# Sparse mixtures: routing two blocks ahead of the scatters, positions in a PSUM bank of their own, two blocks routed in the prologue

## The reference

```
x = x + 0.5 * L0_ffn(layernorm(x))      # gated mixture
x = x + L0_attn(layernorm(x))           # 16 heads, segments of 32 with a memory
x = x + 0.5 * L0_ffn(layernorm(x))      # the gated mixture again, same weights
x = x + 0.5 * L1_ffn(layernorm(x))      # SiLU mixture
x = x + L1_attn(layernorm(x))           # 8 heads in a band
x = x + 0.5 * L1_ffn(layernorm(x))      # the SiLU mixture again
```

```
# L0_ffn, gated (F = 128)
scores = softmax(xt @ gate_w.T)
idx    = top_k(scores + gate_b, 2)                   # weights = scores[idx]
h      = (xt @ w1[e].T + b1[e]) * (xt @ w3[e].T + b3[e])
y      = swiglu(h) @ w2[e].T + b2[e]                 # the shared expert likewise
# L1_ffn, SiLU (I = 512)
gates  = softmax(relu(xf @ Wr1 + br1) @ Wr2 + br2)
tg, ti = top_k(gates, 2);  tg = softmax(tg / 2)
h      = silu(xf @ We1[e] + be1[e]) @ We2[e] + be2[e]   # the shared expert likewise
```

## Time and profile before

| | |
|---|---|
| runs | 2786.85, 2788.24, 2788.27 us; median 2788.24 |
| profiled execution | 2785.44 us, its span 2783.6 us |
| granted TensorE clock, mean | 0.814 of full speed |
| busy: PE | 2066.6 us, 74% of the span |
| busy: DVE | 1942.6 us, 70% |
| busy: ACT | 1387.4 us, 50% |
| busy: POOL | 1102.2 us, 40% |

### The profile page before, as it was taken

How to read it: one execution, slowest core, us unless ns; L and a number is a source line. 1 busy time by engine, 2 the same in 40 slices (tenths; PEclk the granted TensorE clock), 3 DMA queues, 4 the chain that set the end, 5 groups by cost and what they waited for, 6 DMA issues and landing times. The chain is left out here.

```text
span 2783.6 us, 86687 instructions
## 1 busy us (share of the span) xinstructions
PE 2066.6 (74%) x35134; PEld 1660.7 (60%) x35134; DVE 1942.6 (70%) x4609; ACT 1387.4 (50%) x2243; POOL 1102.2 (40%) x885
## 2 busy tenths in 40 slices
PE   3688399999999998569578975755666555549894
PEld 2577378887888887458457974541222233337894
DVE  5788477777777777679774444688999876756443
ACT  1556244444444443346455531367999645436452
POOL 3657245544455543365555651002000222206563
PEclk7789699999999999579879995675555578768997
DMA  4132300000000000023332230003333000021324
GB/s 111 44 100 78 96 2 0 0 0 0 0 0 0 0 0 2 18 68 94 113 96 84 77 97 19 0 0 60 61 59 54 9 2 0 0 69 42 90 77 113
DMA packets 103459, 120.79 MB, mean 43 GB/s; under 512 B 23033, under 2 KB 85097, under 8 KB 102657
## 3 DMA queue, kind: packets, MB, share of 16 engines
q1 hardware_dynamic: 82608, 80.92, 11.9%
q0 software_dynamic: 18176, 37.79, 4.0%
q10 hardware_dynamic: 2512, 0.02, 0.0%
HBM read 60.00 MB, written 46.20 MB: 38 GB/s over the span
## 5 line engine op out<-in xcount | busy, mean ns | idle before, releaser
L2263 DVE CUSTOM_DVE_ANT_0 be_logs<-be_joint,be_logs 128x1024 f32<-128x1024 f32 x256 | 293.3, 1220 | 14.9 <-ACT be_logs L2250 13.9
L2250 ACT ACTIVATE be_logs<-be_joint,b_tiny 128x1024 f32<-128x1024 f32 x256 | 283.9, 1115 | 27.1 <-PE be_joint L2235 19.5
L2235 PE MATMUL be_joint<-be_parts_k,be_parts_q 64*128 64x512 f32 x512 | 202.2, 789 | 116.6 <-DVE be_sums L2263 91.4
L2469 POOL TENSOR_TENSOR bw_kT<-b_knT,b_head_of 128x768 f32<-128x768 f32 x40 | 58.5, 1494 | 454.1 <-SPq L2292 296.5
L405 POOL DMA_INDIRECT d_pairs<-s_y_tile,s_x_tiles x156 | 178.6, 1145 | 120.5 <-DVE s_y_tile L1293 95.9
L1600 POOL TENSOR_TENSOR m_roped_q<-m_raw_q,m_cos 128x1024 f32<-128x1024 f32 x32 | 76.0, 2375 | 368.6 <-ACT m_raw_q L1536 368.6
L2235 PEld LDWEIGHTS be_joint<-be_parts_k,be_parts_q 64*128 64x128 f32 x512 | 73.8, 285 | 244.9 <-DVE be_sums L2263 216.4
L405 POOL DMA_INDIRECT d_pairs<-g_y_tile,g_x_tiles x156 | 154.0, 987 | 97.7 <-ACT g_y_tile L828 73.4
L332 POOL DMA_INDIRECT d_rows<-g_xn,g_slot x128 | 132.6, 1036 | 80.4 <-DVE g_slot L323 44.9
L332 POOL DMA_INDIRECT d_rows<-s_xn,s_slot x128 | 128.7, 1005 | 73.2 <-issue 40.0
L1142 PE MATMUL s_ps_y<-s_down,s_a_tile 128*128 x1248 | 151.7, 275 | 0.0
(11 more groups left out here) (465 smaller groups left out, 6211.4 us busy)
## 6 DMA issues: line engine op xcount, KB each, us to landing
g_x_tiles<-d_rows SPq DMA_DIRECT2D x78, 132.0 KB, 2.1
s_x_tiles<-d_rows SPq DMA_DIRECT2D x78, 132.0 KB, 2.1
d_rows<-d_rows SPq DMA_DIRECT2D x32, 132.0 KB
...
```

The lines of the kernel that those rows point to most:

```text
L2235: last = nc.tensor.matmul(joint_ps[k % DEPTH][:, a, :], parts[b % 2][0][rows, i * P:(i + 1) * P], parts[b % 2][1][rows, half * 512:(half + ...
L2250: nc.scalar.activation(logs[k % DEPTH][:, :, :], joint_ps[k % DEPTH][:, :, :], ACT.Ln, bias=A.tiny[:, :]).then_inc(s.log_ready, 1)
L2263: nc.vector.tensor_tensor_reduce(out=flat, in0=joint_ps[k % DEPTH][:, :, :].rearrange("p a j -> p (a j)"), in1=flat, scale=1.0, scalar=0.0 ...
L2469: last = nc.gpsimd.tensor_tensor(kT[:, h, :, :], A.knT[:, bass.ds(j * GROUP, KEYS), :], A.head_of[:, h:h + 1].unsqueeze(2).broadcast_to([P ...
```

## The change

Positions get a bank of their own: `ps_pos` is `ps_y[1]`, and the shared expert's `below` uses `ps_y[0]` alone. `pe_logits(j)` now waits for `shift_ready` of block j-1 (the logits have been read) instead of its slots, and `pe_positions(j)` for the slots of block j-1. `below(j)` waits for `add_shared(j-1)` instead of `add_shared(j-2)`. Two blocks are routed before the loop instead of one, and in the loop logits, shift, exp, top-2 and count are those of block j+2 while positions, slots and scatters are those of block j+1. DVE's statistics of blocks 4 to 7 come before block 0's top-2, and POOL's power over them before the first scatter. `w_low` of experts 1 and up leaves the loop: some stand after the totals, the others after the addresses. The bias rows are made by POOL (zeros), ACT (two copies) and DVE (one subtraction), in partitions 0 and 32. The totals and the starts come one iteration earlier.

The diff, cut to the shared functions and the gated stage:

```diff
 def pe_transpose(self, pe, j):
-    wait(pe, s.hid_ready, j if j < 2 else j - 1)
+    wait(pe, s.hid_ready, j)
...
 def pe_hidden(self, pe, j):
-    pe.wait_ge(s.x_high, min(j + 2, TRIPS) if j else 1)
+    pe.wait_ge(s.x_high, j + 1)
...
 def pe_logits(self, pe, j):
-    wait(pe, s.slots_ready, j)
+    wait(pe, s.shift_ready, j)
...
+    wait(pe, s.slots_ready, j)
+    pos = r.ps_pos[:, 0:GROUP * E]
...
-    for row in range(2):
+    for row in (0, LOW_ROW):
...
+def pool_bias(self, pool):
+    nc, r, s = self.nc, self.r, self.s
+    nc.gpsimd.memset(r.down_bias[:, :, :].bitcast(F32), 0.0).then_inc(s.bias_step, 1)
+def act_bias(self, act):
+    nc, r, s = self.nc, self.r, self.s
+    act.wait_ge(s.bias_in, 64)
+    act.wait_ge(s.bias_step, 1)
+    for row in (LOW_ROW, 0):
+        nc.scalar.copy(r.down_bias[row:row + 1, :, :], r.bias_rows[row:row + 1, :, :]).then_inc(s.bias_step, 1)
 def dve_bias(self, dve):
-    nc, r, s, d = self.nc, self.r, self.s, self.d
-    dve.wait_ge(s.bias_in, 64)
-    nc.vector.memset(r.down_bias[:, :, :].bitcast(F32), 0.0).then_inc(s.bias_step, 1)
-    nc.vector.tensor_copy(r.bias_high[:, :, :], r.bias_rows[:, :, :]).then_inc(s.bias_step, 1)
-    nc.vector.tensor_scalar(r.bias_part[:, :, :], r.bias_rows[:, :, :], d.row_sign[:, 1:2], None, ALU.mult).then_inc(s.bias_step, 1)
+    nc, r, s = self.nc, self.r, self.s
+    low = r.down_bias[LOW_ROW:LOW_ROW + 1, :, :]
     dve.wait_ge(s.bias_step, 3)
-    nc.vector.tensor_scalar(r.bias_rows[:, :, :], r.bias_high[:, :, :].bitcast(F32), d.row_sign[:, 0:1], None, ALU.mult).then_inc(s.bias_step, 1)
-    dve.wait_ge(s.bias_step, 4)
-    nc.vector.tensor_tensor(r.down_bias[0:2, :, :], r.bias_rows[:, :, :], r.bias_part[:, :, :], ALU.add).then_inc(s.bias_step, 1)
+    nc.vector.tensor_tensor(low, r.bias_rows[LOW_ROW:LOW_ROW + 1, :, :], low.bitcast(F32), ALU.subtract).then_inc(s.bias_step, 1)
...
-    sp.wait_ge(s.bias_step, 5)
+    sp.wait_ge(s.bias_step, 4)
...
-    pe.wait_ge(s.slots_ready, TRIPS)
+    pe.wait_ge(s.shift_ready, TRIPS)
...
-    flat = r.x_tiles[0:2, :, :, :].rearrange("p l h c -> p (l h c)")
-    r.bias_rows, r.bias_part = (flat[:, n * NE * D:(n + 1) * NE * D].rearrange("p (e d) -> p e d", d=D) for n in range(2))
-    r.bias_high = sb("bias_high", [2, NE, D], F32R)
+    r.bias_rows = r.x_tiles[0:LOW_ROW + 1, :, :, :].rearrange("p l h c -> p (l h c)")[:, 0:NE * D].rearrange("p (e d) -> p e d", d=D)
...
+    r.ps_pos = ps_y[1]
...
+    dispatch.pool_bias(pool)
+    dispatch.pool_rstd(pool, 4, 8, 2)
     pool.wait_ge(s.set_up, 4)
     for j in range(TRIPS):
         dispatch.pool_scatter(pool, j)
-        if j == 0:
-            dispatch.pool_rstd(pool, 4, 8, 2)
...
     def below(j):
-        wait(pe, s.x_done, j - 1)
+        wait(pe, s.x_done, j)
         if j == 0:
-            pe.wait_ge(s.bias_step, 5)
-        nc.tensor.matmul(ps_y[j % 2][:, :], d.ones_r[:, :], r.down_bias[:, E, :].unsqueeze(1).broadcast_to([P, GROUP, D]), start=True, stop=False,
+            pe.wait_ge(s.bias_step, 4)
+        nc.tensor.matmul(ps_y[0][:, :], d.ones_r[:, :], r.down_bias[:, E, :].unsqueeze(1).broadcast_to([P, GROUP, D]), start=True, stop=False,
...
         if i < 2:
             pe.wait_ge(s.x_done, TRIPS)
+            pe.wait_ge(s.slots_ready, TRIPS)
...
     dispatch.pe_transpose(pe, 0)
     dispatch.pe_logits(pe, 0)
     dispatch.pe_transpose(pe, 1)
+    dispatch.pe_logits(pe, 1)
     dispatch.pe_positions(pe, 0)
+    dispatch.pe_transpose(pe, 2)
     for j in range(TRIPS):
-        if j + 2 < TRIPS:
-            dispatch.pe_transpose(pe, j + 2)
         if j == 0:
             pe.wait_ge(s.w_low, 1)
         above(j, 0)
-        if j:
-            dispatch.pe_positions(pe, j)
         if j + 1 < TRIPS:
-            dispatch.pe_logits(pe, j + 1)
+            dispatch.pe_positions(pe, j + 1)
         above(j, 1)
-        if j + 1 == TRIPS:
-            dispatch.pe_totals(pe)
         if j:
             below(j - 1)
-    dispatch.pe_starts(pe)
+        if j + 2 < TRIPS:
+            dispatch.pe_logits(pe, j + 2)
+        if j + 3 < TRIPS:
+            dispatch.pe_transpose(pe, j + 3)
+        if j + 2 == TRIPS:
+            dispatch.pe_totals(pe)
+            dispatch.pe_starts(pe)
     dispatch.pe_tables(pe)
...
-    front(0)
-    front(1)
+    parts(0)
+    dispatch.act_second_rows(act, 0)
     dispatch.act_exp(act, 0)
+    parts(1)
+    dispatch.act_second_rows(act, 1)
     w_high(0)
+    dispatch.act_exp(act, 1)
+    dispatch.act_bias(act)
+    parts(2)
+    dispatch.act_second_rows(act, 2)
     for j in range(TRIPS):
+        third(j)
+        sigmoid(j)
+        w_high(j + 1)
         if j + 2 < TRIPS:
-            front(j + 2)
-        third(j)
-        if j + 1 < TRIPS:
-            dispatch.act_exp(act, j + 1)
-        w_high(j + 1)
-        sigmoid(j)
+            dispatch.act_exp(act, j + 2)
+        if j + 3 < TRIPS:
+            parts(j + 3)
+            dispatch.act_second_rows(act, j + 3)
...
         def add_shared(j):
             dve.wait_ge(s.y_full, j + 1)
             x = X[:, j * GROUP:(j + 1) * GROUP, :]
-            nc.vector.scalar_tensor_tensor(out=x, in0=ps_y[j % 2][:, :].rearrange("p (t d) -> p t d", d=D), scalar=0.5, in1=x,
+            nc.vector.scalar_tensor_tensor(out=x, in0=ps_y[0][:, :].rearrange("p (t d) -> p t d", d=D), scalar=0.5, in1=x,
...
     dispatch.dve_stats(dve, 3)
     dispatch.dve_normalise(dve, 1, 2)
     dispatch.dve_shift(dve, 0)
-    dispatch.dve_normalise(dve, 2, 2)
+    for j in range(4, TRIPS):
+        dispatch.dve_stats(dve, j)
     dispatch.dve_top2(dve, 0)
     dispatch.dve_count(dve, 0)
     dispatch.dve_pair(dve, 0)
+    dispatch.dve_normalise(dve, 2, 2)
+    x_low(0)
     dispatch.dve_slots(dve, 0)
-    x_low(0)
+    dispatch.dve_shift(dve, 1)
     w_low(0)
-    x_low(1)
+    dispatch.dve_normalise(dve, 3, 2)
+    dispatch.dve_top2(dve, 1)
+    dispatch.dve_count(dve, 1)
+    dispatch.dve_pair(dve, 1)
     dispatch.dve_bias(dve)
-    for j in range(4, TRIPS):
-        dispatch.dve_stats(dve, j)
     for j in range(TRIPS):
-        if j + 3 < TRIPS:
-            dispatch.dve_normalise(dve, j + 3, rstd_of(j + 3))
+        if j + 1 < TRIPS:
+            x_low(j + 1)
+            dispatch.dve_slots(dve, j + 1)
+        products(j)
         if j + 2 < TRIPS:
-            x_low(j + 2)
+            dispatch.dve_shift(dve, j + 2)
+        elif j + 2 == TRIPS:
+            dispatch.dve_totals(dve)
+            for e in range(1, 4):
+                w_low(e)
+        else:
+            dispatch.dve_tables(dve)
+        if j + 4 < TRIPS:
+            dispatch.dve_normalise(dve, j + 4, 3)
         if j:
-            dispatch.dve_slots(dve, j)
-        if j + 1 < TRIPS:
-            dispatch.dve_shift(dve, j + 1)
-        else:
-            dispatch.dve_totals(dve)
-        if j:
-            activate(j - 1)
-        if j + 1 < TRIPS:
-            dispatch.dve_top2(dve, j + 1)
-            dispatch.dve_count(dve, j + 1)
-            dispatch.dve_pair(dve, j + 1)
-        products(j)
-        w_low(j + 1)
-        if j > 1:
-            add_shared(j - 2)
-    dispatch.dve_tables(dve)
-    activate(TRIPS - 1)
+            add_shared(j - 1)
+        activate(j)
+        if j + 2 < TRIPS:
+            dispatch.dve_top2(dve, j + 2)
+            dispatch.dve_count(dve, j + 2)
+            dispatch.dve_pair(dve, j + 2)
     dispatch.dve_addresses(dve)
-    add_shared(TRIPS - 2)
+    for e in range(4, NE):
+        w_low(e)
     dve.wait_ge(s.table_ready, 1)
     dve.wait_ge(s.w_low, NE)
     experts = tile_values(nc, mybir.EngineType.DVE, r.tile_expert, MAX_TILES, E)
```

More of the change, by code:

```diff
@@ L647, in gated_stage @@
         block = ctx.enter_context(nc.Block())
-        rstd_of = lambda j: 1 if j == 0 else 2 if j < 4 else 3
         @block.sync
@@ L695, in below @@
                 for t in range(GROUP):
-                    last = nc.tensor.matmul(ps_y[j % 2][:, t * D:(t + 1) * D], a[:, t * P:(t + 1) * P], w.w2T[:, E, :], start=False, stop=True,
+                    last = nc.tensor.matmul(ps_y[0][:, t * D:(t + 1) * D], a[:, t * P:(t + 1) * P], w.w2T[:, E, :], start=False, stop=True,
                                             skip_group_check=True)
@@ L783, in w_high, with parts @@
                 nc.scalar.copy(up[:, x, 0, :, :, :], w.w13T[:, :, x, :, :]).then_inc(s.w_high, 1)
-            def front(j):
+            def parts(j):
                 dispatch.act_xnT(act, j)
```

110 lines of the change are left out of this document (55 added, 55 removed).

## The result

| | before | changed |
|---|---|---|
| median of 20 runs each | 2787.63 us (2784.09 to 2789.41) | 2782.68 us (2777.33 to 2788.1) |
| ratio | | 0.9985, 95% interval [0.9978, 0.9992] |
| span of the profiled execution | 2783.6 us | 2780.3 us |

The account below looks back on a forecast made before the run. Four routing stages bound the kernel, with POOL's scatters waiting for slot numbers; gains of 1.4 + 1.0 + 5.6 + 7.0 = 15.0 us off 2785.44 gave 2770.4, and 2.8 more for the median gave 2773 us; range 2754 to 2791.

Parts of the forecast that it names:

- Ahead of the first scatter: Stage start: statistics of all eight blocks before routing make the first scatter 3.8 us later in g, 4.0 in s.
- The period of a block in g: Loop of the gated stages: DVE waits for PE's logits; period 12.9 us, then 11.9 with nothing left to normalise.
- Count 7: End of DVE's count of block 7, from the stage's start; forecast at 101.3 us in g, 91.4 in s.
- the 13.5 that the text gave as a sign of being wrong: Loop of the gated stages: a period under 11.5 or over 13.5 us would show the forecast wrong.
- The fast rival: Gated stages: PE at 2.4 GHz, or logits there early; stage 113.2 us, total 2750 us; chance 0.18.
- The tail of g: Gated stages, from block 7's count to the first tile matmul: 23.4 us, between 21.4 and 25.1.
- The period in s: Loop of the SiLU stages: a cycle through PE, ACT and DVE of 9.8 us per block.
- never waits: SiLU stages: POOL, needing 10.45 us a block against a period of 9.8, would not wait for slots.
- The floor of POOL: SiLU stages: first scatter 23.4 us, plus 83.6 for 64 scatters, plus 5.3 behind them, gives 112.3 us.
- The tail of s: SiLU stages, from block 7's count to the first tile matmul: 22 us, giving 113.4 from the start.
- the slower one: PE stays at 1.2 GHz while it routes: 14 us lost, 2802 us, from a g period of 13.3; chance 0.15.
- the one in which scatters still wait in s: SiLU stages: a cycle of 11.1 us, not 9.8, takes their gain away, total 2786 us; chance 0.17.

Follow-up runs that it names:

- experiment 5: Changed kernel with PE's logits(j+2) right behind above(j,0) in g and w_low rows of six and two in s; 2761.71 us (1 run).
- experiment 3: Changed kernel with g1's small loads ahead of SP's pads, and in s block 0 exp(2) and positions(2) earlier; 2788.18 us (1 run).
- experiment 6: Changed kernel without rows of w_low in s and with g1's small loads ahead of the pads; 2774.96 us (5 runs), ratio to before 0.9958.
- experiment 8: Changed kernel: logits, shift, small loads and exp(2) earlier, no w_low rows, statistics of blocks 4 to 7 behind slots(0); 2751.05 us, ratio to before 0.9863.
- experiment 4: Changed kernel with PE's logits(j+2) behind above(j,0) and DVE's shift(j+2) ahead of products(j) in g, exp(2) earlier in s; 2761.23 us (1 run).
- experiment 2: Changed kernel with each w_low of the rows waiting for the end of the one before, leaving short gaps; 2790.49 us (1 run).
- experiment 1: Changed kernel with w_low(j) back in DVE's loop in g and s, one alone left behind the addresses; 2776.32 us (1 run).

## Why the prediction was wrong

Three steps of it failed. In s, POOL was to wait for no slots, and it waited 3.6 us in s0 and 4.6 in s1; and the rows of `w_low` were priced as DVE's time alone, while they also held two scatters, 3.8 and 3.9 us a stage. In g1, the tail was taken from g0, and SP's list made it 1.9 us longer. Besides, DVE's tail in s was put 1.4 us too short. Part by part:

*Ahead of the first scatter: right.* Forecast 3.8 us later in g and 4.0 in s; measured 4.3, 4.3, 2.7 and 4.5. The gap ahead of block 1 went in all four stages.

*The period of a block in g: right.* Forecast 12.9; measured, for blocks 3 to 6, 12.2 to 13.1 in g0 and 13.1 to 13.4 in g1, by the logits' wait that the text named, and experiment 5 shows that this place in PE's list is the cause. Count 7 was forecast at 101.3 and came at 100.1 and 102.5. It held narrowly: in the executions of experiments 3 and 6 the same code of g0 had periods up to 13.6, over the 13.5 that the text gave as a sign of being wrong. The fast rival's time of a g stage (113) is nearly reached by the order alone (115.8 and 116.3) and reached with the other edits (experiment 8), by the second of the rival's reasons, logits that are there early, and not by the first, a PE at the high level: experiment 4 gained 6.7 us in g0 at the same granted 0.75.

*The tail of g: right for g0, wrong for g1.* Forecast 23.4 from count 7 to the first tile matmul; g0 had 23.4. In g1 it was 25.3. The step that failed is taking g0's tail for both gated stages: only g1 has the small loads and the wait for them on SP's list, which the text left out. The tail was 1.9 us longer than forecast (by experiment 3 SP's list costs 2.1), and count 7 came 1.2 later: 3.1 in all.

*The period in s: right, its consequence wrong.* Forecast 9.8; measured 9.8 to 10.0 from count 3 on, and 10.4 and 11.1 ahead of it. But count 2 was put 14.1 us behind count 1, at 42.4, and the sentence that POOL "never waits" does not follow: slots come 2.7 us behind the count, and POOL was done with block 1 at 44. Count 2 came 16.1 and 16.2 behind count 1 (at 44.1 and 44.5), while exp(2) stood behind four `expand`, a `w_high` and a table load on ACT, and the `expand` waited for a PE that was granted about half of full speed (windows at the end of this section). POOL waited 3.6 us there and 1.0 ahead of block 3 (s1). The place of exp(2) is not all of it: with exp(2) moved, in experiment 4, POOL still waited 3.3 us in s1, for positions(2).

*The floor of POOL, 83.6 us for 64 scatters, in s: wrong.* The tail's `w_low` were priced as DVE time only. Each row also held one scatter, 2.83 - 0.96 = 1.9 us and 2.93 - 0.96 = 2.0. In s1: 23.7 to the first scatter, 61.9 busy without the holds and 64 x 0.3 between the scatters, waits 3.6 + 1.0, holds 3.9, 5.1 behind the end: 118.4, as measured. The forecast had 112.3. Of these 6.1 us the waits are 4.6 and the scatters only 1.4 (85.0 for 83.6), as the forecast's mean of 1.005 us was taken from a kernel that had longer scatters of its own, and hid part of the holds.

*The tail of s: sized too short.* +22 was forecast from count 7; what experiment 2 leaves less its gaps is 23.4, from a count 7 that was itself 3 us late. POOL's end was 5.1 and 6.1 us too early and DVE's about 4 and 5, by different errors, and so the forecast of 113.4 looked safe from two sides.

The miss is 4.0 + 5.0 in s and 3.1 in g1, less 1.2 in g0: 10.9 us of stage time. Experiment 6 took out the rows and SP's wait, left POOL's waits in s1 nearly as they were (4.1 us), and found 2775. No rival was right: the slower one asked for a g period over 13.3 and a charged tail in s; the one in which scatters still wait in s had the right place, but wanted a cycle of 11.1 us.

s0 gained 2.3 us in experiment 4 and 2.2 in 5, and 6.3 in 6, s1 nothing in 4 and 5. Windows over the loop's first steps of s0 and then of s1, in the kernel of experiment 6, show the same code with PE granted 0.79 in the one and 0.50 in the other (columns as in the earlier trace rows):

```profile
1423.60:1438.60 15.00, 12.22 (x65) 8.70 (x65) 8.99 (x53) 11.75 (x19) 11.65 (x12) 0.79 0.16 55
2509.50:2524.50 15.00, 11.82 (x34) 8.32 (x35) 7.54 (x38) 9.23 (x14) 11.34 (x13) 0.50 0.17 56
```

Count 2 came at 41.1 in the one and 44.5 in the other, POOL waited 0.5 us ahead of block 2 and not 3.6, and s0 took 111.1. In the changed kernel s0 had 0.53 there and s1 0.50, and in the kernel before the same stretches, 24.9 to 39.9 us after the stage's start, had 0.94 and 0.92. In the experiments s0's stretch had 0.77 to 0.79 in 4, 5 and 6, and 0.50 to 0.53 in the others. Some 3 us of a SiLU stage go with this level (111.1 here, 114.4 in experiment 1), and the forecast did not price it; that the change itself lowered the level is argued from these windows and was not tried apart. Why s0 gets the higher level early in the executions of 4, 5 and 6 and not in others stays open; no experiment was aimed at it.
